# Four-layer transformer stack on one core: four split-product slots, gates in place, another order of the last eight down steps

## The reference

```python
x = x + L0_xattn(layernorm(x), ctx); x = x + L0_ffn(layernorm(x))   # routed tokens, width 704
x = x + L1_xattn(layernorm(x), ctx); x = x + L1_ffn(layernorm(x))   # 64 experts of 64, top 8, + shared 64
x = x + L2_xattn(layernorm(x), ctx); x = x + L2_ffn(layernorm(x))   # self-attention, 8 experts of 176, top 2, + shared 704
x = x + L3_xattn(layernorm(x), ctx); x = x + L3_ffn(layernorm(x))   # 16 experts of 176, top 4, + shared 176
```

```python
y += (silu(h @ w_gate[e]) * (h @ w_up[e]) * gate_of_token[e]) @ w_down[e]     # layers 0 to 2
y += (silu((h @ w1[e]) * (h @ w3[e])) * gate_of_token[e]) @ w2[e]             # layer 3
```

## Time and profile before

| what | us |
|---|---|
| median of three runs | 1272.53 |
| span of the profiled execution | 1269.1 |
| PE busy in it | 1177.4 (93%) |
| DVE busy | 878.3 (69%) |
| ACT busy | 508.2 (40%) |
| POOL busy | 378.7 (30%) |

### The profile page before, as it was taken

How to read it: one execution, slowest core, us unless ns; L and a number is a source line. 1 busy time by engine, 2 the same in 40 slices (tenths; PEclk the granted TensorE clock), 3 DMA queues, 4 the chain that set the end, 5 groups by cost and what they waited for, 6 DMA issues and landing times.

```text
span 1269.1 us, 21808 instructions
## 1 busy us (share of the span) xinstructions
PE 1177.4 (93%) x8429; PEld 771.4 (61%) x8429; DVE 878.3 (69%) x1718; ACT 508.2 (40%) x1141; POOL 378.7 (30%) x397
## 2 busy tenths in 40 slices
PE   6889999999889999999899989889999888899997
PEld 4664658999645666566566745554655565456665
DVE  3777976676676666666757797987666676766666
ACT  3423360111233333333353345653334343555553
POOL 1540215656303333333203420001333242233332
PEclk9889999999999999999999997999999989999999
DMA  4030141000054444445330000002443200344342
GB/s 147 2 158 21 49 142 40 1 1 2 11 212 121 117 117 116 117 117 121 105 144 1 18 1 1 2 2 81 121 119 111 65 18 1 90 120 121 120 126 84
DMA packets 41544, 97.19 MB, mean 77 GB/s; under 512 B 5446, under 2 KB 18246, under 8 KB 39392
## 3 DMA queue, kind: packets, MB, share of 16 engines
q1 hardware_dynamic: 41440, 95.79, 24.8%
HBM read 94.35 MB, written 1.42 MB: 75 GB/s over the span
## 4 chain that ended last, share of the span: by engine, by line
PE 75%; DVE 14%; ACT 4%; issue 3%; DMA 2%; POOL 1%; SPq 0%; DVEq 0%; POOLq 0%; ACTq 0%
PE PS L1445 9%; PE PS L1446 9%; PE PS L1447 9%; PE PS L1490 4%; PE PS L1492 4%; PE PS L1491 4%; PE PS L1063 3%; PE PS L1081 2%; PE PS L1258 2%; PE PS L1049 2%; PE PS L1051 2%; PE PS L1050 2%; ACT arena L2286 2%; PE PS L2209 1%; DVE small L569 1%
## 5 line engine op out<-in xcount | busy, mean ns | idle before, releaser
L1670 POOL TENSOR_TENSOR arena<-arena,m_g 128x512 f32<-128x512 f32 x142 | 182.1, 1284 | 405.8 <-DMA m_g<-gate_rows 227.2
L1445 PE MATMUL PS<-arena 128*128 128x512 f16 x608 | 231.0, 380 | 3.5 <-DVE arena L1605 3.0
L1447 PE MATMUL PS<-arena 128*128 128x512 f16 x608 | 231.1, 380 | 0.0
L1446 PE MATMUL PS<-arena 128*128 128x512 f16 x608 | 231.1, 380 | 0.0
L1490 PE MATMUL PS<-arena 128*128 128x256 f16 x608 | 165.8, 273 | 11.7 <-DVE arena L1625 8.9
L1492 PE MATMUL PS<-arena 128*128 128x256 f16 x608 | 165.7, 273 | 0.0
L1491 PE MATMUL PS<-arena 128*128 128x256 f16 x608 | 165.7, 273 | 0.0
L1565 ACT ACTIVATE arena<-PS 128x512 f32<-128x512 f32 x112 | 66.8, 597 | 234.8 <-PE PS L1447 224.4
L1608 DVE SCALAR_TENSOR_TENSOR arena<-arena,PS 128x512 f32<-128x512 f32 x112 | 76.9, 686 | 120.0 <-ACT arena L1565 119.5
L1625 DVE TENSOR_TENSOR arena<-arena 128x512 f16<-128x512 f32 x142 | 112.4, 791 | 3.2 <-ACT arena L1575 3.2
L1447 PEld LDWEIGHTS PS<-arena 128*128 128x128 f16 x608 | 59.6, 98 | 72.1 <-issue 0.6
(11 more groups left out here) (282 smaller groups left out, 2250.1 us busy)
## 6 DMA issues: line engine op xcount, KB each, us to landing
w_stage<-in_up SPq DMA_DIRECT2D x80, 256.0 KB, 2.8
m_g<-gate_rows SPq DMA_DIRECT2D x70, 256.0 KB, 4.2
arena<-in_heads SPq DMA_DIRECT2D x16, 1088.0 KB, 5.3
w_stage<-in_down SPq DMA_DIRECT2D x80, 128.0 KB, 4.0
m_g<-gate_rows SPq DMA_DIRECT2D x17, 512.0 KB, 3.9
m_g<-gate_rows SPq DMA_DIRECT2D x6, 448.0 KB, 4.3
m_g<-gate_rows SPq DMA_DIRECT2D x6, 384.0 KB, 4.0
m_g<-gate_rows SPq DMA_DIRECT2D x6, 320.0 KB, 4.3
```

Of the source, the lines that this page charges most:

```text
L1445: pe.matmul(to, w_hi, x_hi, start=(k == 0), stop=False)
L1446: pe.matmul(to, w_lo, x_hi, start=False, stop=False)
L1447: ins = pe.matmul(to, w_hi, x_lo, start=False, stop=(k == KT - 1))
L1670: pool.tensor_tensor(m_c[:, st % 2, :], m_b[:, st % LAG, :], m_g[:, st // 2 % 2, st % 2, :], ALU.mult).then_inc(s.c, 1)
```

## The change

It touches the four feed-forwards:

- **Four slots.** `hid` has four slots instead of two (`HIDS = 4`), used in the order in which the down steps come. ACT waits for the down step four places back instead of two.
- **Gates in place.** `m_c` is gone: POOL writes the gated product back into `m_b`. It waits for the product and the gate rows alone. DVE no longer waits for POOL before it overwrites a slot of `m_b`. The gate rows are asked for two tiles ahead: the first two together, then those of c + 2 where those of c were.
- **Order.** The last eight down steps come as F-7, F-5, F-3, F-8, F-1, F-6, F-4, F-2. F-7, F-5 and F-3 belong to the first half of the tokens, F-1 to both, F-8, F-6, F-4 and F-2 to the second. `down_halves` (F-1) is thus fourth from the end and raises `y_ps` for banks 4 and 5; the very last step raises it for 6 and 7. ACT and DVE split in the same order, one step earlier in total: two products in the last step, the first of them ahead of its tanh.
- **Down weights.** The last three tiles' down weights have a place of their own (`dn_x`), so that their split doesn't wait for down steps.
- Loads of weights of several layers now count on shared semaphores (`weights`); the waits are for the same loads.

```diff
+HIDS = 4
-        m_c, at = take(at + 1024, [2, 512])
-        hid, at = take(at, [2, 2, 4, P], F16)
+        dn_x, _ = take(at, [4, 2, D], F16)
+        hid, at = take(at + 1024, [HIDS, 2, 4, P], F16)
...
             for c in range(f.tiles):
                 if c + 5 < f.tiles:
                     sp_up(n, c + 5)
-                if c < f.gated:
-                    if c == 0:
-                        sp.wait_ge(s.rows, 16 * n)
-                    sp_gates(n, c)
+                if c == 0 and f.gated:
+                    sp.wait_ge(s.rows, 16 * n)
+                    sp_gates(n, 0)
+                    sp_gates(n, 1)
+                if c + 2 < f.gated:
+                    sp_gates(n, c + 2)
                 if c >= 2:
                     sp_dn(n, c)
...
-            for st in range(f.steps - LAG, f.steps - 1):
-                down(st)
-            down_halves(f.steps - 1)
+            for st in in_order(n)[f.steps - LAG:]:
+                (down_halves if st == f.steps - 1 else down)(st)
...
-            if c >= 2:
+            if 2 <= c < FFNS[n].tiles - 3:
                 nc.scalar.wait_ge(s.down, downs0(n) + 2 * c - 2)
...
+        def in_order(n):
+
+            F = FFNS[n].steps
+            return list(range(F - 8)) + [F - 7, F - 5, F - 3, F - 8, F - 1, F - 6, F - 4, F - 2]
+
+        def place(n, st):
+            return in_order(n).index(st)
+
+        def finished(n, st):
+
+            final, order = FFNS[n].steps - 1, in_order(n)
+            if st < final:
+                return [order[st - LAG + 1]] if st >= LAG - 1 else []
+            return [order[final - LAG + 1], order[final - LAG + 2]] if st == final else [order[st - LAG + 2]]
...
             def high(st):
-                if st >= 2:
-                    act.wait_ge(s.down, downs0(n) + st - 1)
+                if place(n, st) >= HIDS:
+                    act.wait_ge(s.down, downs0(n) + place(n, st) - HIDS + 1)
...
-                dve_slot_free(n, st)
...
                 pool.wait_ge(s.prod, f.steps0 + st + 1)
                 if st % 2 == 0:
                     pool_gates(n, st // 2)
-                if st >= 2:
-                    pool.wait_ge(s.lo, f.steps0 + st - 1)
-                pool.tensor_tensor(m_c[:, st % 2, :], m_b[:, st % LAG, :], m_g[:, st // 2 % 2, st % 2, :], ALU.mult).then_inc(s.c, 1)
+                p = m_b[:, st % LAG, :]
+                pool.tensor_tensor(p, p, m_g[:, st // 2 % 2, st % 2, :], ALU.mult).then_inc(s.c, 1)
```

More of the change, by code:

```diff
@@ L1467, in down_halves @@
                             rows, i = slice(P // 2 * h, P // 2 * (h + 1)), 4 * h + j
-                            ins = pe.matmul(PS[:, 4 + i // 2, (i % 2) * D:(i % 2 + 1) * D], hid[rows, 0, p, j, :], dn_w[rows, c % 2, w, :],
-                                            start=False, stop=(p == 1 and i % 2 == 1))
+                            ins = pe.matmul(PS[:, 4 + i // 2, (i % 2) * D:(i % 2 + 1) * D], hid[rows, hid_slot(n, st), p, j, :],
+                                            dn_tile(n, c)[rows, w, :], start=False, stop=(p == 1 and i % 2 == 1 and h == 0))
                             if p == 1 and j % 2 and h == 0:
                                 ins.then_inc(s.y_ps, 1)
-                ins.then_inc(s.y_ps, 2)
+                ins.then_inc(s.down, 1)
             def gates_turned():
@@ L1480, in down @@
             def down(st):
-                c, h = st // 2, st % 2
+                c, h, last = st // 2, st % 2, st == f.steps - 2
                 if h == 0:
                     pe.wait_ge(s.dn_lo, f.tiles0 + c + 1)
-                pe.wait_ge(s.lo, f.steps0 + st + 1)
-                w_hi, w_lo = (dn_w[:, c % 2, a, :] for a in range(2))
+                pe.wait_ge(s.lo, f.steps0 + place(n, st) + 1)
+                w_hi, w_lo = (dn_tile(n, c)[:, a, :] for a in range(2))
                 for j in range(4):
@@ L1488, in down @@
                     to = PS[:, 4 + i // 2, (i % 2) * D:(i % 2 + 1) * D]
-                    h_hi, h_lo = (hid[:, h, a, j, :] for a in range(2))
+                    h_hi, h_lo = (hid[:, hid_slot(n, st), a, j, :] for a in range(2))
                     pe.matmul(to, h_hi, w_hi, start=(c == 0 and i % 2 == 0), stop=False)
                     pe.matmul(to, h_hi, w_lo, start=False, stop=False)
-                    ins = pe.matmul(to, h_lo, w_hi, start=False, stop=False)
-                ins.then_inc(s.down, 1)
+                    ins = pe.matmul(to, h_lo, w_hi, start=False, stop=(last and i % 2 == 1))
+                    if last and j % 2:
+                        ins.then_inc(s.y_ps, 1)
+                if not last:
+                    ins.then_inc(s.down, 1)
             for st in range(f.steps):
@@ L1590, in act_ffn @@
                     act_up_hi(n, c + 1)
-                if h == 1 and st >= LAG - 1:
-                    act_dn_hi(n, (st - LAG + 1) // 2)
+                if due and due[-1] % 2 == 0:
+                    act_dn_hi(n, due[-1] // 2)
                 if st < f.steps and product_first(n, st):
@@ L1622, in low @@
             def low(st):
[L1623 removed]
+                dve.wait_ge(s.hi, f.steps0 + place(n, st) + 1)
                 if gated(n, st):
[L1625 removed]
+                    dve.tensor_tensor(hid_part(n, 1, st), m_b[:, st % LAG, :], hid_part(n, 0, st), ALU.subtract).then_inc(s.lo, 1)
                 else:
[L1627 removed]
+                    dve.scalar_tensor_tensor(hid_part(n, 1, st), m_b[:, st % LAG, :], plain_down_scale(n, st), hid_part(n, 0, st),
                                              ALU.mult, ALU.subtract).then_inc(s.lo, 1)
[L1630 to L1631 removed]
+            for st in range(f.steps + LAG - 2):
+                c, h, due = st // 2, st % 2, finished(n, st)
+                if len(due) == 2:
+                    dve_dn_lo(n, due[0] // 2)
+                    low(due[0])
                 if begun <= st < f.steps:
```

101 lines of the change are left out of this document (51 added, 50 removed).

## The result

| kernel | median us | spread | ratio to before, interval |
|---|---|---|---|
| before | 1270.96 | 1267.27 to 1273.1 | |
| after | 1260.2 | 1255.94 to 1261.04 | 0.9921 [0.99, 0.9942] |

The change makes the kernel 0.8% faster, 10.8 us; measured once more it was 0.9925 [0.9903, 0.9947]. The profiled execution of after has a span of 1258.0 against 1269.1, at a mean granted clock of 0.981 against 0.976. The page of after: engine totals, then the groups of the gate multiply (L1670 before, L1697 now), the first down matmul and the split (L1625 before, L1651 now).

The account below looks back on a forecast made before the run. TensorE bounds the kernel (75% of the chain, busy throughout a feed-forward's body). Terms -11.1 -3.8 +6.9 +3.4 = -4.6 us gave span 1264.5 and run 1268, range 1259 to 1278.

Parts of the forecast that it names:

- Drains: Nine down steps behind each feed-forward's last up product: shorter by 3.7, 3.7, 3.3 in FFN1 to FFN3, 0.4 in FFN0.
- the stall that was put at 0.95: End of FFN1: the last gate multiply holds DVE's split of F-5, so PE waits 0.95 us once.
- Rival 3: End of the feed-forwards: DVE or the last down weights' load becomes the bound, half the gain left; 1273.5 us, chance 0.14.
- Tails: Behind the last down steps: earlier first-half sums save 0.8 behind FFN1, 1.0 behind FFN2, 2.0 at the end.
- Starts: First tiles of FFN1 to FFN3: four multiplies in a row delay the first split; +1.1, +0.95, +1.3, together +3.4 us.
- Bodies: Middle tiles: POOL's paired multiplies hold DVE's splits and stall PE; FFN1 +3.6, FFN2 +0.1, FFN3 +3.2, together +6.9 us.
- L1625 ends at 3.7 plus that start: FFN1's middle tiles: the split ends then, PE wants it at 2.94, so PE stalls 0.82 plus the start.
- 0.2 before L1532: FFN1's middle tiles: POOL's second multiply starts this many us before the up-weight split and holds it a whole multiply.
- The loop through SP: FFN1's middle tiles: L1532 and SP's gate request 0.9 us late delay the next multiply; repeats in two or three tiles.
- Rival 1: Middle tiles pay nothing, POOL's pair stays within DVE's slack: -11.5 us, 1261; chance 0.25.
- the mark that I gave for it: Middle tiles: PE's waits for the split stay under 2 us, against 6.9 in the forecast.
- The rule weighed there: GpSimd and two-SBUF-input VectorE operations lock each other out for whole instructions: keeps +6.9 and 1268; free overlap gives 1261.

Follow-up runs that it names:

- the small multiply: Changed kernel with POOL's gate multiply cut to 16 of 512 columns, all waits kept; 1251.79 us, ratio 0.9867.
- the paced kernel: Changed kernel with one more wait: in the feed-forward body POOL's multiply waits for the split of five steps before; 1260.98 us, ratio 0.9917.

## Why the prediction was right, and where it was not

1268 was predicted, in a range of 1259 to 1278; 1260.2 came, inside but 1.2 from its edge, below the forecast's own range (1263 to 1273) and on the side of faster, which had 0.39 against 0.50 for the same. The 7.8 between are 3.6 in the stretches (5), 1.6 in the kernel before, whose median came out as 1270.96 and not 1272.53, and 2.6 that no term had (6).

1. **Drains**, -3.7, -3.7, -3.3 and -0.4 predicted: -3.55, -3.5, -3.0 and -0.6 measured. One step in each of the first two drains takes 2.08 instead of 1.31, the stall that was put at 0.95. Rival 3 (half of the drain's gain) is out. Of the reasons, two slots in the changed kernel give 13.5 and four slots without gates in place 14.3: both parts are needed for 12.8, and POOL's wait was the larger one.
2. **Tails**: -2.0 at the end was -2.2; behind FFN1 -0.8 was -0.97; behind FFN2 -1.0 was -1.6.
3. **Starts**, +1.1 and +0.95 for FFN1 and FFN2: +1.3 and +1.0. The step is visible: PE waits 1.03, where the earlier trace rows had 0.19 and the prediction 1.3.

```profile
379.69 5.59 POOL L1697 TENSOR_TENSOR arena<-arena,m_g 128x512 f32<-128x512 f32 x4 [29.80 <-DMA m_g<-gate_rows]
...
382.40 1.75 DVE L1651 TENSOR_TENSOR arena<-arena 128x512 f16<-128x512 f32 x1
...
384.30 0.27 PE L1495 MATMUL PS<-arena 128*128 128x256 f16 x1 [1.03 <-DVE arena L1651]
```

4. **Bodies**: the mechanism was right, the size in FFN1 was not. POOL's multiplies come in pairs, and the small multiply shows that they are the cause. L1539 is over 1.2 us in 11 of 24 tiles of FFN1, not in most, and over 0.8 in 20. FFN1's body had +3.6 and paid +1.1; FFN2's had +0.1 and paid that. FFN3's start and body together had +4.5 and paid 3.4 and 4.3 in the two profiles, of it 1.7 and 0.8 in the second down step; the rest is scattered over its body, as I had it. In FFN1 the first matmuls of the down steps stand 3.90 apart, and only 4 of 55 such distances are longer, by 0.12, 0.51, 0.08 and 0.36. The longest, POOL, DVE and PE:

```profile
447.68 2.95 POOL L1697 TENSOR_TENSOR arena<-arena,m_g 128x512 f32<-128x512 f32 x2 [6.47 <-DMA m_g<-gate_rows]
...
447.75 1.75 DVE L1539 SCALAR_TENSOR_TENSOR arena<-w_stage,arena 128x512 f16<-128x512 f32 x1
449.42 1.75 DVE L1651 TENSOR_TENSOR arena<-arena 128x512 f16<-128x512 f32 x1
...
451.23 0.28 PE L1495 MATMUL PS<-arena 128*128 128x256 f16 x1 [0.35 <-DVE arena L1651]
```

   The pair starts 0.07 before L1539, and the split ends at 451.17, which is 3.49 behind the pair's start. The step that failed is "L1625 ends at 3.7 plus that start": it counted multiply, split, multiply as 1.27 + 0.69 + 1.27, but the pair with L1539 in its middle takes 2.94 or 2.95. So the stall is the start plus some 0.6, not plus 0.82: four tiles with pairs at -0.47, -0.07, -0.50 and -0.22 stall by 0.12, 0.51, 0.08 and 0.36. And only 5 of 24 tiles from 400 us on have a pair later than -0.6 (the fifth starts 0.06 behind L1539, which it doesn't hold), where the prediction put every second or third tile. With 0.82 in place of 0.6 the pair starts of this trace would give some 2.2 us (an estimate), so about half of what the prediction had too much is the length of the pair and the rest is how seldom it comes late. The prediction's "0.2 before L1532" is such a matter too: it is right for a first multiply at -1.5, but the tile of the earlier trace rows, at 403.62, leaves 0.64. The loop through SP that it described is there: behind a tile with a long L1539 (1.54, 1.80) the next pair comes late (-0.47, -0.07), and behind a short one (0.83, 0.68) early (-1.25, -2.02).
5. **The sum**: predicted -4.6. Measured in the stretches: -8.2, the own 7.2 and FFN1's tail of 1.0. The 3.6 between them: starts and bodies +7.3 instead of +10.3 (3.0, of it 2.5 FFN1's body), tails 1.0 more, drains 0.5 less. Two profiles of after differ by 1.0 in this.
6. **The rest**: the profiles differ by 4.3 more and the medians by 2.6 (1.8 the second time) more than the change accounts for; no term had this. In the profiles it goes with the granted clock behind FFN1. Without it and with the median of before as forecast the time would have been 1264.4. That the range still covered 1260.2 is luck: nothing in the sum spoke of either. Rival 1 (1261) named the time but not the way: there the bodies paid nothing, and the mark that I gave for it, PE's waits for the split in the bodies under 2 us, is met all the same. PE's 6.6 us hold 1.0, 0.7 and 2.0 at the first down steps of FFN1, FFN2 and FFN3, 0.6 in each of two drains and 1.6 in the bodies, while the bodies grew by 5.6: the distances of the down steps show what the wait table doesn't.

The rule weighed there, from the Trainium skill, "SBUF — State Buffer", section "SBUF: two separate sides": a GpSimd operation and a VectorE operation with two SBUF inputs exclude each other for the whole instruction, the first to start going first. The small multiply bears out that they exclude each other. It doesn't bear out "whole" for the duration that the trace shows: a pair of multiplies alone takes 2.50 and with L1539 between them 2.94 or 2.95, so a DVE operation of 0.69 us holds POOL by only 0.44. By the trace, not by the page, FFN1's body comes out.

## What to carry to other kernels

Where two engines take turns on a shared resource at the end of a loop, list all links of the ring: each of the two that were cut here gave less alone (16.3 to 14.3, or to 13.5 with the other) than both (12.8). Then price each cut over the whole kernel as well: the gates in place shortened the drains and cost more than that in starts and bodies. What contention inside a loop costs hangs on a threshold, the time at which the bounding engine wants the result: of 24 pairs in FFN1's body four stalled PE. An early request in a queue shared with other loads needs its release to be early as well, or all behind it stands: it cost 195 us in one kernel and 3.2 in a single tile of another.

## What the hardware showed that I had not expected

- The stretch behind FFN1, the same work in every kernel, takes 233 to 241 us with TensorE's granted clock (mean 1.00 to 0.96). Both profiles of before have it long (240.6 and 239.1), both of after short (234.8), and two kernels that differ from after by one POOL wait have 239.2. So a profile can differ by 5 us in a stretch that the edit doesn't reach. Why the clock stays at 1.2 GHz in a busy stretch of one and not of the other is open.
- One kernel's executions differ by 19 us (1260.5 to 1279.25) with a mean granted clock from 0.989 to 0.969. Read at one clock, differences of 2 to 5 us show that medians of 8 or 12 executions hide.
- POOL's pairs cost DVE 44 us of busy time (878.3 to 922.1), of which 7.3 reach PE in the starts and bodies.
- Own stretches and medians part: the paced kernel has 3.6 us less in its own stretches than after and the same median; at an equal clock it has 2.2 less.
